# A graph layer's edge stage: PE turns a batch's inputs one step ahead, and source rows come by broadcast loads

## The reference

```python
deg = jnp.maximum(jnp.zeros((n,)).at[dst].add(1.0), 1.0)
edge_weight = (deg[src] * deg[dst]) ** -0.5
edge_msg = relu(edge_attr @ W1e + b1e) @ W2e + b2e
messages = (x[src] + edge_msg) * edge_weight[:, None]
agg = segment_sum(messages, dst, num_segments=n)
combined = (1.0 + gin_eps) * x + agg
h = relu(combined @ W1n + b1n) @ W2n + b2n
out = h + x
out = out * rsqrt(mean(out * out, axis=-1) + RMS_EPS) * rms_w
return layernorm(x + out)
```

## Time and profile before

| | us |
|---|---|
| median of 3 runs | 2106.02 |
| lowest, highest | 2101.01, 2118.94 |
| the profiled execution | 2100.82 |
| its span, first to last instruction | 2098.9 |
| mean granted PE clock over the span | 0.831 of full |

### The profile page before, as it was taken

The page is one execution under the profiler, slowest core; times in us unless marked ns, Lnnn a source line. Parts: engine busy times, 40 slices in busy tenths (PEclk is TensorE's granted clock), DMA queues, the critical chain, the costliest instruction groups (busy, mean ns, idle before and its releaser), DMA issues. The chain is left out here.

```text
span 2098.9 us, 36900 instructions
## 1 busy us (share of the span) xinstructions
PE 1448.9 (69%) x8715; PEld 1031.3 (49%) x8836; DVE 1264.9 (60%) x4446; ACT 1106.9 (53%) x3992; POOL 1296.4 (62%) x2150
## 2 busy tenths in 40 slices
PE   2115982766666666667567576665799999999994
PEld 1002542444444444344445354444577777777773
DVE  2004994544444454445445454454499999999997
ACT  2004970333333333333333343334599999999997
POOL 7771005255655556565555555566388989889887
PEclk7556996787878788787777787787899999999997
DMA  7886001111111111111111111130447677676673
GB/s 278 301 303 276 12 0 35 29 51 40 43 40 41 39 52 42 39 42 38 42 39 48 44 42 41 43 118 30 157 187 275 251 264 276 245 268 267 255 268 147
DMA packets 60152, 262.72 MB, mean 125 GB/s; under 512 B 17323, under 2 KB 19699, under 8 KB 35632
## 3 DMA queue, kind: packets, MB, share of 16 engines
q1 hardware_dynamic: 34642, 218.18, 27.7%
q0 software_dynamic: 25136, 43.60, 7.1%
q10 hardware_dynamic: 302, 0.20, 0.0%
HBM read 141.53 MB, written 128.09 MB: 128 GB/s over the span
## 5 line engine op out<-in xcount | busy, mean ns | idle before, releaser
L564 POOL DMA_INDIRECT agg_scratch<-scaled,sca_i x390 | 389.3, 998 | 417.4 <-ACT scaled L695 319.9
L557 POOL DMA_INDIRECT xs<-in_x,src_x x391 | 381.1, 975 | 284.9 <-DVE fin_i L877 165.2
L816 DVE TENSOR_SCALAR picks<-highq,high_no 128x512 f16<-128x512 f16 x686 | 246.1, 360 | 445.1 <-remote 344.0
L1098 PE MATMUL bank<-digits,picks 128*128 128x256 f16 x2744 | 383.5, 291 | 60.9 <-issue 55.5
L1098 PEld LDWEIGHTS bank<-digits,picks 128*128 128x128 f16 x2744 | 285.7, 105 | 124.9 <-issue 72.8
L1116 PE MATMUL bank<-eaT,w1e 64*128 64x512 f32 x196 | 148.7, 848 | 282.4 <-ACT eaT L669 180.4
L598 POOL TENSOR_SCALAR xsc<-xn,rms 128x128 f32<-128x128 f32 x784 | 277.8, 372 | 87.4 <-issue 38.8
L669 ACT ACTIVATE eaT<-bank 64x512 f32<-64x512 f32 x98 | 57.6, 588 | 467.4 <-remote 368.0
L899 DVE SCALAR_TENSOR_TENSOR picked<-iota_h,src_lo,bank 128x256 f32<-128x256 f16 x392 | 185.1, 472 | 148.1 <-remote 141.6
L611 POOL TENSOR_SCALAR on<-z,neg_mean,rstd 128x128 f32<-128x128 f32 x568 | 245.9, 443 | 0.9 <-issue 0.9
L1076 PE MATMUL bank<-oh_hi,steps 128*128 128x512 f16 x392 | 144.7, 408 | 146.4 <-issue 101.4
(11 more groups left out here) (157 smaller groups left out, 2633.6 us busy)
## 6 DMA issues: line engine op xcount, KB each, us to landing
agg_scratch<-zeros SPq DMA_DIRECT2D x48, 1024.0 KB
xn<-in_x SPq DMA_DIRECT2D x48, 1024.0 KB
out<-on SPq DMA_DIRECT2D x48, 1024.0 KB, 4.9
ag<-agg_scratch SPq DMA_DIRECT2D x47, 1024.0 KB, 6.8
ea<-in_edge_attr SPq DMA_DIRECT2D x21, 512.0 KB
xs<-in_x,src_x POOLq DMA_INDIRECT x391
agg_scratch<-scaled,sca_i POOLq DMA_INDIRECT x390
ea<-in_edge_attr SPq DMA_DIRECT2D x3, 448.0 KB
```

The costliest lines, as they stand in the source:

```text
L557: pool.indirect_dma_start(out=xs[:, b % XS, j, :], out_offset=None, in_=x, in_offset=bass.IndirectOffsetOnAxis(ap=src_x[:, t:t + 1], axis= ...
L564: pool.indirect_dma_start(out=agg_rows, out_offset=bass.IndirectOffsetOnAxis(ap=sca_i[:, t:t + 1], axis=0), in_=scaled[:, b % SR, j, :], i ...
L816: return dve.tensor_scalar(picks[:, s, c, :], highq[:, q, :], high_no[:, c:c + 1], None, ALU.is_equal)
L1098: last = pe.matmul(ps[half][:, j * 2 * P:(j + 1) * 2 * P], picks[:, s, c, e:e + P], digits[:, c, :, :].rearrange("p d l -> p (d l)"), star ...
```

## The change

Source rows no longer go through PE and ACT. `high_b` is stored once to a tensor in HBM (`src_high_scratch`), and SP loads it back with the source row repeated for all 128 partitions, four batches at a time, into one of two slots of `highq` (`row_loads`); DVE waits for that load in place of ACT's copy. The spreading matmul, its weights' identity in f16, the copy and their semaphores go. PE turns the inputs of batch b+1 within step b (`turn_inputs`), and ACT copies them within step b (`take_inputs`), so the matmul with `w1e` is the first of PE's step; the transposes stand behind it and ahead of both halves of the picks. ACT's `he` moves from behind the weighings to the head of its step.

```diff
+high_d = nc.dram_tensor("src_high_scratch", (CW * P,), f16)
-        highq = sb("highq", [P, HQ, W], f16)
+        highq = sb("highq", [P, 2, EB * W], f16)
...
+            sp.wait_ge(high_ready, 1)
+            sp.dma_start(high_d[:].rearrange("(b c) -> b c", c=W), high_b[:, :]).then_inc(high_out, 16)
+
+            def row_loads(b):
+                n = min(EB, BATCHES - b * EB) * W
+                need(sp, picks_ready, (b - 1) * EB)
+                sp.dma_start(highq[:, b % 2, 0:n],
+                             high_d[b * EB * W:b * EB * W + n].rearrange("(o c) -> o c", o=1).partition_broadcast(P)
+                             ).then_inc(highq_in[b % 2], 16)
...
+            sp.wait_ge(high_out, 16)
             for b in range(2):
+                row_loads(b)
                 edge_loads(b)
             zero(ZERO_FIRST, BLOCKS)
...
             for b in range(2, -(-BATCHES // EB)):
                 edge_loads(b)
+                row_loads(b)
...
+            def take_inputs(b, u):
+                act.wait_ge(eaT_done, at(b + 1))
+                need(act, h_done, b - 1)
+                act.activation(eaT[:, u % 2, :], ps[2][0:ED, :], ACT.Copy).then_inc(eaT_ready, 1)
...
             def edge_step(b, u):
                 if live(b, BATCHES):
-                    act.wait_ge(eaT_done, at(b + 1))
-                    need(act, h_done, b - 1)
-                    act.activation(eaT[:, u % 2, :], ps[2][0:ED, :], ACT.Copy).then_inc(eaT_ready, 1)
+                    act.wait_ge(h_done, at(b + 1))
+                    need(act, m_done, b - 1)
+                    act.activation(he[:, u % 2, :], ps[3][:, :], ACT.Relu, bias=b1e_c[:, 0:1]).then_inc(h_ready, 1)
...
-                if live(b + 2, BATCHES):
-                    spread_high(b + 2, (u + 2) % HQ)
-                if live(b, BATCHES):
-                    act.wait_ge(h_done, at(b + 1))
-                    need(act, m_done, b - 1)
-                    act.activation(he[:, u % 2, :], ps[3][:, :], ACT.Relu, bias=b1e_c[:, 0:1]).then_inc(h_ready, 1)
+                if live(b + 1, BATCHES):
+                    take_inputs(b + 1, u + 1)
...
                 if picking:
-                    dve.wait_ge(highq_ready, b + 2)
+                    dve.wait_ge(highq_in[(b + 1) // EB % 2], ((b + 1) // (2 * EB) + 1) * 16)
...
+            def turn_inputs(b, u):
+                pe.wait_ge(ea_in[u // EB % 2], at(ea_loaded(b)))
+                apart(pe, pe_passed)
+                for j in range(TB):
+                    last = pe.transpose(ps[2][0:ED, j * P:(j + 1) * P], ea[:, u // EB % 2, u % EB * TB + j, :],
+                                        ident[:, :])
+                last.then_inc(eaT_done, 1)
...
                     pe.matmul(ps[3][:, :], w1e[:, :], eaT[:, s, :], start=True, stop=True).then_inc(h_done, 1)
-                if live(b + 2, BATCHES):
-                    spread_high(b + 2)
+                if live(b + 1, BATCHES):
+                    turn_inputs(b + 1, u + 1)
+                if live(b, BATCHES):
+                    pick_counts(b, s, 0)
```

More of the change, by code:

```diff
@@ L128, in build @@
         ones_b = sb("ones_b", [P, P], bf16)
-        ident_h = sb("ident_h", [P, P], f16)
         w1e = sb("w1e", [ED, D])
@@ L281, in build @@
         high_ready = sem("high_ready")
-        high_spread = sem("high_spread")
+        high_out = sem("high_out")
         high_hot = sem("high_hot")
@@ L630, in _ @@
             act.activation(iota_h[:, :], iota_i[:, :], ACT.Copy).then_inc(iota_set, 1)
-            act.wait_ge(ident_s, 1)
-            act.activation(ident_h[:, :], ident[:, :], ACT.Copy).then_inc(ident_hot, 1)
             act.wait_ge(src_parts, 1)
@@ L637, in _ @@
             act.activation(high_b[:, :], ps[2][0:BATCHES, :], ACT.Copy).then_inc(high_ready, 1)
[L639 to L645, removed]
             act.wait_ge(dst_cols, 1)
@@ L699, in _ @@
             act.wait_ge(wts_in, 16 * WEIGHTS)
+            take_inputs(0, 0)
             run(act, BATCHES, SR, edge_step, tail=5, head=3, peel=1)
@@ L813, in _, with pick_column @@
             dve.tensor_copy(cnt[:, 512:HIGH], ps[1][:, 0:HIGH - 512]).then_inc(cnt_ready, 1)
-            def pick_column(s, q, c):
-                return dve.tensor_scalar(picks[:, s, c, :], highq[:, q, :], high_no[:, c:c + 1], None, ALU.is_equal)
+            def pick_column(b, c):
+                return dve.tensor_scalar(picks[:, b % 2, c, :], highq[:, b // EB % 2, b % EB * W:(b % EB + 1) * W], high_no[:, c:c + 1], None, ALU.is_equal)
             def pick_columns(b):
-                dve.wait_ge(highq_ready, b + 1)
+                dve.wait_ge(highq_in[0], 16)
                 for c in range(HCH):
-                    last = pick_column(b % 2, b % HQ, c)
+                    last = pick_column(b, c)
                 last.then_inc(picks_ready, 1)
@@ L1057, in _ @@
             last.then_inc(high_turned, 1)
-            pe.wait_ge(high_ready, 1)
-            pe.wait_ge(ident_hot, 1)
-            def spread_high(b):
-                need(pe, highq_ready, b)
-                pe.matmul(ps[2][:, :], ident_h[0:BATCHES, bass.ds(at(b), 1)].to_broadcast([BATCHES, P]), high_b[:, :],
-                          start=True, stop=True).then_inc(high_spread, 1)
-            for b in range(2):
-                spread_high(b)
             def count_step(b, u):
@@ L1105, in edge_step @@
                 if live(b, BATCHES):
-                    pe.wait_ge(ea_in[u // EB % 2], at(ea_loaded(b)))
-                    need(pe, eaT_ready, b)
-                    pe.wait_ge(highq_ready, at(b + 2) if live(b + 1, BATCHES) else BATCHES)
-                    apart(pe, pe_passed)
-                    for j in range(TB):
-                        last = pe.transpose(ps[2][0:ED, j * P:(j + 1) * P], ea[:, u // EB % 2, u % EB * TB + j, :], ident[:, :])
-                    last.then_inc(eaT_done, 1)
-                    pick_counts(b, s, 0)
                     pe.wait_ge(eaT_ready, at(b + 1))
@@ L1137, in _ @@
             pe.wait_ge(lists_ready, 1)
+            turn_inputs(0, 0)
             run(pe, BATCHES, 2 * EB, edge_step, tail=1, peel=EA_TAIL // (2 * EB) + 1)
```

6 lines of the change are left out of this document (2 added, 4 removed).

## The result

The changed kernel takes 2081.75 us (median of 4 runs, 2081.48 to 2083.53), the kernel before beside it 2108.08 (4 runs, 2101.01 to 2118.94): a ratio of 0.9894, 95% interval 0.985 to 0.994. The forecast was 2048, 58 us under the 2106 of before; the measured difference is 26 us, 1.1%. The direction was right, and 2081.75 lies between 1975 and 2125, at the upper edge of the forecast's own 2008 to 2082; the size was less than half of it. The two profiled executions are only 17.3 us apart (2100.82 and 2083.53): that of before was just under the shortest of its runs, that of after the longest of its four.

A forecast was written before the change was run, and what follows sets the result against it. The edge stage was taken as bound by turns of POOL bursts, held PE releases and restarts through ACT. Terms -54 - 3 - 1 + 3 = -55 us from 2100.8 gave 2046, named 2048; own range 2008 to 2082, wider range 1975 to 2125.

The forecast's parts named there:

- The hold: Edge stage: while POOL issues indirect DMAs, PE's work and releases are held, from some 7 us after POOL's start.
- The restart: Edge stage, from the release through ACT's step to POOL: 5.65 us before, 3.58 after, 2.07 less for a long wait.
- The sum: Edge stage: POOL's 285 us of waits shrink; -54 us, taken as the middle of two ways of counting, -37 and -72.
- (a): Edge stage: every burst holds two batches, 45 waits of 5.5 us, 248 us in place of 285: -37 us.
- (b): Edge stage: pattern of turns stays; 19 long waits save 2.07 us each, 47 others 0.7 each: -72 us.
- Start of the stage: Between 330 and 401 us: each step loses the spreading matmul and one of six releases; -3 us, between 0 and -12.
- Counting: Before the edge stage: ACT starts counting up to 2.5 us sooner, counting ends at PE's pace; -1 us, 0 to -2.5.
- The loads: SP's added highq loads in the edge stage: never late, but might lengthen the hold; +3 us, at worst +23.
- Some ten us of delay there meet no one: 0 us: SP's queue before the edge stage: the store and its wait delay first edge loads and zero blocks at no cost.
- No change: Edge stage rival, chance 0.20: the hold is the budget, earlier restart takes 2.1 us from PE; about 2100 us.
- more: Edge stage rival, chance 0.17: a third batch gets into each burst, 30 waits of 5.5 us; -120, 1980 us.
- slower: Edge stage rival, chance 0.13: bursts merge but PE isn't done at their end, 45 waits of 7.6 us; +57, about 2155.

The follow-up runs named there:

- b0_before: The kernel before, unchanged, run again for its trace, in a set where POOL had no gaps over 1 us in the edge stage: 1647.28 us.
- x2: The changed kernel with ACT's scaled moved directly behind he, with POOL's pauses present: 2031.67 us beside the kernel before at 2105.41, ratio 0.9651.
- second set with pauses: Later runs where POOL again paused in the edge stage: the changed kernel, unchanged, 2083.32 us in one run, beside the kernel before at 2108.52.
- e2: The kernel before with only PE's and ACT's order changed, spreading kept: 2088.04 us beside 2108.52 with POOL's pauses; 1650.55 us (1.0008) without.

## Why the prediction was right and wrong

**The hold** is real on these traces and bounds the stage: PE does 48 counting matmuls in 120 us with POOL issuing and 667 in 115 us without, and in the runs that do not have it the same program takes 457 us less. What is held is above all PE's increments, as the counting and the edge stage show; its recorded matmuls thin out only late in a burst. "Until 2 us after its end" is right in the edge stage alone: in the counting the last late increment comes at 185.4 us, 20 us behind POOL's last gather. What the chip does is not settled. It is not POOL's issuing alone, for b0_before issues as densely with PE 13.28 us of 14 busy; there the rule of the Trainium skill, "SBUF — State Buffer", section "SBUF: two separate sides", that PE never waits, agrees with the trace, and with pauses the trace goes against it, or something outside that rule holds PE.

**The restart**: 3.58 us forecast, 3.51 measured. Right, and x2, in which it is 1.77 us, shows that a shorter one shortens the pauses.

**The sum** is where it failed.
- The term that failed is the edge stage's: -54 us forecast, -17 measured (285.0 to 268.1 us of POOL's waits). Taking the middle of (a) and (b) is 17 us of the miss. (b), "the pattern of turns stays", is refuted: all bursts became two batches. (a) said so in words and in number (45 waits near 5.5 us; 46 gaps of 5.71), and it alone should have been the forecast. The signs that the prediction names mix the two as well: 45 pauses of 5.5 us are 248 us and can't be a wait "near 230".
- The other 20 us are in (a)'s own -37. It counted 45 waits of 5.5 us, 248 us; the 268.1 are 46 of 5.71 and 5.5 us of waits under 1 us, for which the sum had nothing (before had 5.8 us of them among its 285.0). So one pause more is some 6 us, 0.2 us on each some 9, and the short waits 5.5.
- What both ways missed is how uneven before was: 20 gaps paid the long restart, and the other 36, at 3.66 us, were cheaper than the even pauses that replaced them. The merging took back 17 of the 37 us that the shorter restart won. (The prediction's 19 waits over 7 us with 145 us in all are 18 with 138 in the trace.)
- **Start of the stage**, -3: measured +0.4 at the first scatter. **Counting**, -1: ACT starts it 2.7 us sooner and ends it at 303.9 us, before at 303.7; the earlier start is lost again.
- **The loads**, +3: nothing to be seen in after's trace; scatters, gathers and picks are as they were. No run has them alone with pauses.
- **"Some ten us of delay there meet no one: 0 us"** is right only with the hold, which puts the first scatter over 180 us behind the fill. Without it the fill's end is what the first scatter waits for, and the same delay costs 5 us.

**The rivals.** "No change", with as many pauses and the same total, is refuted by 46 gaps for 56 and 262.6 us for 283.0; but something of its kind is at work, since x2 won 47 us of the 80 that its restart was shorter by. No third batch per burst came through in after, and its merged bursts did restart on time, so neither "more" nor "slower" held. The median difference, 26 us, agrees with the 25 of the second set with pauses and is more than the profiled pair's 17; before's runs scatter over 18 to 22 us, after's over 2.

**Open**: what holds PE's increments, and whether it goes by the chip, the time or something else; whether their number matters then; what the loads do alone under it. Between e2 and the changed kernel lie 5 us in one run each, too few to name their share.

## What to carry to other kernels

Where a stage goes in turns of burst and pause, list the pauses by the instruction at which the restarting engine goes on, and count the batches per burst. The gain is the sum of the pauses now less their number times their length afterwards, not the cut in the restart times their number: that would have given 46 x 2.07 = 95 us here, and 20 were won. When the pattern can go two ways, forecast one of them, not the mean. Let the engine that restarts the bound one do that first and the rest of its step afterwards: moving four ACT instructions within their step was worth twice what the whole change was. And ask of a delay that "meets no one" what hides it, since in another run that cover may be gone: here it was worth 5 us.

## What the runs showed of the hardware

One program, the kernel before, takes 1649 us beside some runs and 2106 us beside others, and all runs of one set agree. What decides it is not known. The difference is in the two stages in which POOL issues indirect DMAs beside PE's work: ACT's counting ends at 144.5 or 303.7 us and the edge stage takes 806 or 1075 us, while the node rows behind take 622 us in both.

With pauses, PE's semaphore increments come late while POOL issues: 40.8 us behind the matmul in the counting, one in 22.5 us, and one in some 7 us in a burst of the edge stage; without pauses 0.02 us behind it. Nothing of the kind shows for ACT's increments in the same stretch: PE starts on `steps` 0.55 us after ACT does. In the edge stage a waiting ACT is let through about 2.2 us after POOL's burst ends (medians of 2.1 to 2.4 in before, after, e2 and x2), with PE's matmuls some 0.7 us apart late in a burst; behind the gathers of the counting it took 20 us.

POOL itself is no slower with pauses. Its 128 gathers beside the counting end at 165.6 us with them and at 176.2 without, 1.26 and 1.34 us each.

The granted clock does not explain it: in 713 to 727 us it is 0.76 in b0_before and 0.75 in the earlier trace rows, at 13.28 and 4.28 us of busy PE. Over longer stretches it is lower where PE stands more, 0.79 for the edge stage of before and 0.87 for that of b0_before.
